# A decoder layer on one core: the context's keys and values in plain fp32 instead of three fp32r passes

## The reference

```python
kv = (key_value_states @ Wkv).reshape(B, K, 2, H, D)      # context [32, 375, 256] @ [256, 512], fp32
k = kv[:, :, 0].transpose(0, 2, 1, 3)
v = kv[:, :, 1].transpose(0, 2, 1, 3)
scores = jnp.einsum('bhsd,bhkd->bhsk', q, k) + bias
attn = jax.nn.softmax(scores, axis=-1)
out = jnp.einsum('bhsk,bhkd->bshd', attn, v)
return out @ Wo
```

## Time and profile before

| What | us |
|---|---|
| median of 3 runs (lowest, highest) | 1374.55 (1373.27, 1375.71) |
| the profiled execution | 1373.25 |
| its span in the trace | 1371.6 |
| TensorE busy | 1270.6 |
| POOL, DVE, ACT busy | 856.5, 832.5, 718.6 |

### The profile page before, as it was taken

One profiled execution on the slowest core, in us unless ns is written; L12 is line 12 of the kernel. 1 busy time (PEld: TensorE's weight loads), 2 busy tenths in 40 slices (PEclk: granted clock), 3 DMA queues, 4 the chain that ended last, 5 costly groups with the idle time before them and its releaser, 6 DMA issues. The chain is left out here.

```text
span 1371.6 us, 41710 instructions
## 1 busy us (share of the span) xinstructions
PE 1270.6 (93%) x13316; PEld 1069.9 (78%) x13317; DVE 832.5 (61%) x3821; ACT 718.6 (52%) x1827; POOL 856.5 (62%) x1597
## 2 busy tenths in 40 slices
PE   5499999999999999999999999996199999999993
PEld 3378888878878888878878878874099999999993
DVE  2257767777677767777677767765444444444441
ACT  2256666566656666566656666564044444444440
POOL 4276787778777787778777777775423544444431
PEclk9799999999999999999999999999599999999997
DMA  8910111100101111110101111000366332222224
GB/s 163 174 46 23 30 38 34 30 30 27 45 27 30 31 38 34 30 31 27 44 27 30 30 33 36 12 16 27 114 197 175 55 50 50 46 46 46 47 44 122
DMA packets 47327, 73.30 MB, mean 53 GB/s; under 512 B 6832, under 2 KB 34032, under 8 KB 47088
## 3 DMA queue, kind: packets, MB, share of 16 engines
q1 hardware_dynamic: 31408, 45.74, 12.5%
q0 software_dynamic: 15744, 25.31, 9.3%
HBM read 46.90 MB, written 27.80 MB: 54 GB/s over the span
## 5 line engine op out<-in xcount | busy, mean ns | idle before, releaser
L458 POOL TENSOR_SCALAR arena<-arena,mC 112x375 f32<-112x375 f32 x512 | 299.7, 595 | 155.0 <-DVE mC L839 153.1
L839 DVE CUSTOM_DVE_ANT_0 arena<-bank_S,arena 112x375 f32<-112x375 f32 x512 | 254.9, 545 | 113.8 <-PE bank_S L586 84.0
L1070 POOL DMA_INDIRECT acc<-y,xb x64 | 116.5, 1821 | 210.4 <-DVE y L1214 155.3
L464 POOL TENSOR_SCALAR arena<-arena,mF 112x112 f32<-112x112 f32 x512 | 202.2, 417 | 8.1 <-DVE mF L827 8.1
L693 ACT ACTIVATE arena<-bank_B 128x224 f32<-128x224 f32 (+6 forms) x260 | 101.1, 389 | 114.1 <-PE bank_B L567 54.2
L693 ACT ACTIVATE arena<-bank_A 128x224 f32<-128x224 f32 (+3 forms) x252 | 98.7, 392 | 109.2 <-PE bank_A L567 54.3
L1201 DVE SCALAR_TENSOR_TENSOR hT<-bankU,gub,gate 128x128 f32<-128x128 f32 x256 | 72.1, 344 | 101.7 <-PE bankU L1110 99.0
L721 ACT ACTIVATE pTC<-bank_Q 126x336 f32<-126x336 f32 x256 | 115.2, 450 | 34.2 <-PE bank_Q L595 24.1
L586 PE MATMUL bank_S<-arena 32*112 32x376 f32 x1024 | 116.0, 522 | 17.9 <-DVE mC L839 17.6
L1110 PE MATMUL bankG<-xbT,gwb 128*128 128x128 f32 x1024 | 126.6, 277 | 1.0 <-ACT gwb L1157 1.0
L1110 PE MATMUL bankU<-xbT,uwb 128*128 128x128 f32 x1024 | 126.0, 277 | 0.0
(11 more groups left out here) (196 smaller groups left out, 2714.2 us busy)
## 6 DMA issues: line engine op xcount, KB each, us to landing
arena<-in_l_ctxT SPq DMA_DIRECT2D x32, 378.0 KB
xb<-xs POOLq DMA_DIRECT2D x64, 129.0 KB, 3.5
arena<-in_L_ffn_gate_w SPq DMA_DIRECT2D x8, 512.0 KB
arena<-in_L_ffn_up_w SPq DMA_DIRECT2D x8, 512.0 KB
arena<-in_L_ffn_down_w SPq DMA_DIRECT2D x8, 512.0 KB
arena<-in_x SPq DMA_DIRECT2D x32, 112.0 KB, 2.0
acc<-arena SPq DMA_DIRECT2D x32, 112.0 KB, 1.9
out<-acc SPq DMA_DIRECT2D x4, 896.0 KB, 9.3
```

Source lines behind the costliest of these rows:

```text
L458: pool.tensor_scalar(z[n % NZ][:, 0:T], z[n % NZ][:, 0:T], -1.0, mC[:, n:n + 1], ALU.mult, ALU.add).then_inc(s_u, 1)
L464: m = pool.tensor_scalar(sF[r][:, j, :], sF[r][:, j, :], -1.0, mF[:, r, j:j + 1], ALU.mult, ALU.add)
L839: dve.tensor_tensor_reduce(out=z[n % NZ][:, 0:T], in0=bank[f"S{r}"][0:S, 0:T], in1=nbias[:, n, :], scale=1.0, scalar=3.0e38, op0=ALU.add, ...
L1070: pool.indirect_dma_start(out=acc[:, :], out_offset=bass.IndirectOffsetOnAxis(ap=xb[x][:, D + 1:D + 2].bitcast(I32), axis=0), in_=y2[x % 2 ...
```

## The change

Each product of the context projections is one fp32 matmul on the loaded context and the loaded weights. The tiles `cT` and `wkv`, their semaphores, the steps `ch` and `cl` and `split_weights` are gone. TensorE waits for the context's load itself, and SP waits for the four projections of the item two before. The table `PERIOD` is a new one: a different order in every engine, and items up to 5 periods ahead instead of 4.

```diff
-t9@-1 e7@-1 pv1 xn@2 x1 su2@2 xn2 su0@2 v0c e2@-1 ln2 t11@-1 u10 e4@-1 t10@-1 nrmc@-2 oncc@-2 t12@-1 t15@-1
...
+u15@-1 p7@1 t5 oc3@-2 pf@-1 v0@2 e1@-1 e0@-1 onc p5@1 wo@2 u1 u2 e3@-1 rcA@-2 nrm@1 v@3 e7@-1 t11 otc t8
...
-            cT = [s1(f"cT_{part}", [P, DC, TPAD], F32R) for part in ("high", "low")]
-            wkv = [s1(f"wkv_{part}", [P, DC, 2 * D], F32R) for part in ("high", "low")]
-            PASSES = ((0, 0), (1, 0), (0, 1))
...
                         elif step == "Lc" and b >= 2:
-                            sp.wait_ge(s_cl, b - 1)
+                            for w in ("k0", "k1", "v0", "v1"):
+                                filled_wait(sp, w, b - 2)
                             load_c(b)
...
                     def keys(o, b, B_, F_):
                         for c in range(DC):
-                            for u, w in PASSES:
-                                m = pe.matmul(B_[:, 0:T + 1], wkv[w][:, c, o * P:(o + 1) * P], cT[u][:, c, 0:T + 1],
-                                              start=(c == 0 and (u, w) == PASSES[0]), stop=(c == DC - 1 and (u, w) == PASSES[-1]))
+                            m = pe.matmul(B_[:, 0:T + 1], wkv_in[:, c, o * P:(o + 1) * P], cin[b % 2][:, c, 0:T + 1],
+                                          start=(c == 0), stop=(c == DC - 1))
...
                             for c in range(DC):
-                                for u, w in PASSES:
-                                    m = pe.matmul(B_[0:TP, k * D:(k + 1) * D], cT[u][:, c, t * TP:(t + 1) * TP],
-                                                  wkv[w][:, c, D:2 * D], start=(c == 0 and (u, w) == PASSES[0]),
-                                                  stop=(c == DC - 1 and (u, w) == PASSES[-1]))
+                                m = pe.matmul(B_[0:TP, k * D:(k + 1) * D], cin[b % 2][:, c, t * TP:(t + 1) * TP],
+                                              wkv_in[:, c, D:2 * D], start=(c == 0), stop=(c == DC - 1))
...
                         elif step in ("k0", "k1"):
-                            pe.wait_ge(s_cl, b + 1)
+                            pe.wait_ge(s_c[b % 2], 16 * (b // 2 + 1))
...
-                        elif step == "ch":
-                            act.wait_ge(s_c[b % 2], 16 * (b // 2 + 1))
-                            if b:
-                                for w in ("k0", "k1", "v0", "v1"):
-                                    filled_wait(act, w, b - 1)
-                            copy(cT[0][:, :, :], cin[b % 2][:, :, :], s_ch)
...
-                            dve.wait_ge(s_ch, b + 1)
-                            dve.tensor_tensor(cT[1][:, :, :], cin[b % 2][:, :, :], cT[0][:, :, :].bitcast(F32),
-                                              ALU.subtract).then_inc(s_cl, 1)
```

More of the change, by code:

```diff
@@ L66 @@
 PERIOD = """
-t9@-1 e7@-1 pv1 xn@2 x1 su2@2 xn2 su0@2 v0c e2@-1 ln2 t11@-1 u10 e4@-1 t10@-1 nrmc@-2 oncc@-2 t12@-1 t15@-1
-t14@-1 t13@-1 S0@1 x2Tc p8 su3@2 Lc@1 x2@-2 v1c ln3@-2 u1@1 e5@-1 ch@1 x3T@-1 e6@-1 oc0@-1 su1@2 q2m sm2@1
-e11@-1 p10 sm0@1 sm3@1 qk@3 vc@1 e9@-1 xTc@2 sT0@2 p14 x3@-2 rt@-1 sm1@1 S1@1 t1 sT3@2 t3 sT1@2 k0@2 sE2@1 p15
-pvS@2 p12 oc1@-1 e8@-1 t0 x3Tc@-2 pv2 t2 u0@1 e10@-1 p13 sE0@1 u3@1 p3@1 e14@-1 qkc@2 sE3@1 re@-2 cl@1 sE1@1
-lg@-2 ot@2 pv3 p1@1 sc@-2 p0@1 e15@-1 on@2 pf@-1 S2@1 rcA@-2 p7@1 wo@2 p2@1 k1@2 ln1@3 u4@1 v0@2 otc u7@1
-rs1@4 km@3 p4@1 u2@1 S3@1 u6@1 u5@1 onC u8@1 p6@1 k0c@1 t4 t7 p5@1 oTc@1 x2T@2 Lx@3 rs2@2 e12@-1 woc t5 u11@1
-v1@2 u9@1 oc2@-1 S4@3 t6 pv0@1 nrm@1 u15@1 q2@2 e13@-1 e3 oc3@-1 p11@1 u14@1 e1 u13@1 rcB@-2 onc@1 st@-3 v@3
-e0 xT@4 k1c@1 rs3 p9@1 pfD@-2 u12@1 sT2@3 t8
+u15@-1 p7@1 t5 oc3@-2 pf@-1 v0@2 e1@-1 e0@-1 onc p5@1 wo@2 u1 u2 e3@-1 rcA@-2 nrm@1 v@3 e7@-1 t11 otc t8
+pfD@-2 v0c e5@-1 S3@1 xT@4 vc@1 xTc@2 p6@1 oncc@-2 onC e6@-1 p4@1 v1@2 e4@-1 v1c xn2 t10 t9 u0 woc p10@1 u7
+x2Tc u4 e10@-1 oc0@-1 p11@1 e11@-1 u5 S4@3 x2T@2 km@2 q2m x1@1 nrmc@-1 e8@-1 pv0@1 q2@2 u6 p8@1 x3@-2 k0@3
+sT0@3 sE0@1 k0c@1 e9@-1 sE1@1 ln2@1 xn@3 t13 sc@-3 oc1@-1 t15 e14@-1 pv1@1 rs1@4 x3Tc@-2 e13@-1 p9@1 sT1@3
+S0@2 t14 p14@1 x3T u9 p13@1 oc2@-1 pv2@1 qkc@2 sE3@1 u11 qk@4 t12 sT3@3 re@-2 u10 x2@-1 e12@-1 rt p12@1 S1@2
+ln3@-1 rs2@1 sT2@3 e15@-1 sE2@1 p15@1 k1@3 sm0@2 u8 k1c@1 pvS@3 p2@2 sm1@2 p1@2 u14 sm3@2 rcB@-2 sm2@2 t2@1
+Lc@2 pv3@1 t3@1 rs3@-1 u13 t1@1 t0@1 lg@-1 ln1@5 su0@2 Lx@5 oTc@1 su1@2 t4@1 ot@3 e2 su3@2 p0@2 S2@2 t7@1 u12
+on@3 st@-2 su2@2 p3@2 u3@1 t6@1
 """
@@ L290, in decoder_layer @@
             s_pool = sem("pool_constants_ready")
-            s_wkv = sem("context_weights_split")
             s_fb = sem("bias_rows_filled")
@@ L302, in decoder_layer @@
             s_xn2 = sem("xn2_ready")
-            s_ch = sem("context_high_ready")
-            s_cl = sem("context_low_ready")
             s_u = sem("cross_scores_shifted")
@@ L625, in _ @@
                             pe.wait_ge(s_late, 16 * NLATE)
-                        if b == 0 and step in ("k0", "k1", "v0", "v1"):
-                            pe.wait_ge(s_wkv, 1)
                         B_, F_ = fill_wait(pe, step, b), fill_sem(step, b)
@@ L893, in set_up @@
                         link(dve.tensor_scalar(padf[:, :], iota[:, 0:E], float(R), rowf[:, :], ALU.mult, ALU.add))
-                    def split_weights():
-                        dve.wait_ge(s_late, 16 * NLATE)
-                        link(dve.tensor_copy(wkv[0][:, :, :], wkv_in[:, :, :]))
-                        dve.tensor_tensor(wkv[1][:, :, :], wkv_in[:, :, :], wkv[0][:, :, :].bitcast(F32),
-                                          ALU.subtract).then_inc(s_wkv, 1)
                     for step, b in steps:
@@ L923, in _ @@
                             statistics(1, x1[b % NX][:, :])
-                        elif step == "cl":
-                            if b == 0:
-                                split_weights()
-                            dve.wait_ge(s_ch, b + 1)
-                            dve.tensor_tensor(cT[1][:, :, :], cin[b % 2][:, :, :], cT[0][:, :, :].bitcast(F32),
-                                              ALU.subtract).then_inc(s_cl, 1)
                         elif step == "nrmc":
```

## The result

| kernel | median, us | range, runs | span of the profiled run | clock |
|---|---|---|---|---|
| before | 1374.08 | 1373.27 to 1375.71, 4 | 1371.6 | 0.969 |
| after | 1401.32 | 1399.12 to 1402.19, 4 | 1399.9 | 0.965 |

The ratio is 1.0191, 95% interval [1.018, 1.0203]: 27 us slower. Forecast were 1385 us and a range up to 1400. The sign was right, the size was less than half of what came, and the range missed by 1.3 us.

A forecast was written before the change was run, and what follows sets the result against it. TensorE was taken to bound the first stage. 31 items at +0.40 us gave 12.4; with - 1.7 + 0.3 at the start, +11.0 us, so 1385 us. Its own range was 1381 to 1391, the wider one 1377 to 1400.

The forecast's parts named there:

- ScalarE's and VectorE's copies: ACT's 32 copies of 0.84 us and DVE's 32 subtractions of 0.95 us lie beside a full TensorE; removal worth 0.
- the bare fp32 prices: Context steps on TensorE in plain fp32: key step 1.27 us, value steps 1.73 and 0.87 us.
- the borrowed 0.19 at the projection: Projection before the last value step shows 0.68 us for 0.87; the 0.19 us come back in the new order.
- DVE's 3 us for the fifth x: At the start DVE stands 3 us for the fifth x; booked at +0.3 us, at most +3.
- the moved waits in SP's queue: Context load waits for the four projections of the item two before; worth 0.
- What plain fp32 costs: Context products on TensorE: 5.14 us in fp32 against 4.70 for fp32r passes, 0.44 us more an item.
- The order: Walk through one period's 49 groups: others 23.32 us, context 5.14, together 28.46; +0.39, taken as +0.40 an item.
- The start, -1.7 + 0.3: A key step and transposes vanish in the stall before 67 us, -1.7 us; DVE's wait for x, +0.3.
- Rival 1: Context steps: no switch saved between kinds of products, so +0.95 us an item, 1401 us; chance 0.09.
- Rival 2: New order stalls TensorE: late DVE at the normalised heads, 0.3 us an item, 1394 us; chance 0.10.
- Rival 3: TensorE is not the bound; its full rows hide waits that longer products fill, 1374 us; chance 0.08.
- Even distances: TensorE rows of one kind equally far from the next start, 0.87 us for projections, taken to prove the bound.

The follow-up runs named there:

- 11: Kernel before's order with plain fp32, ScalarE's context copy put back into a tile nobody reads; period 28.60 us, ratio to before 1.0092.
- 12: Kernel before's order with plain fp32, VectorE's subtraction put back into a tile nobody reads; period 28.57 us, ratio to before 1.0095.
- 3: Changed kernel with ScalarE's last self exponential of an item moved ahead of a cross exponential; period 28.79 us, ratio to before 1.0149.
- 6: Changed kernel, self exponential first, mask-group scores moved right ahead of the first cross values; 1394.64 us, ratio to before 1.0142.
- run 1: Plain fp32 in the order of the kernel before; 1391.61 us, period 28.60 us, ratio to before 1.0095, timed again 1.010.
- 5: Changed kernel, self exponential first, two pairs of steps on tiles of 32 made neighbours again; period 29.09 us, ratio to before 1.024.
- run 8: Kernel before with the thirteenth head's transposes moved ahead of the self values; period 28.03 us, ratio to before 0.9991.
- run 2: Kernel before with its three fp32r passes, put in the new order; period 28.75 us, ratio to before 1.0132.
- 7: Kernel before with two neighbouring pairs of steps on tiles of 32 parted; period 29.31 us, ratio to before 1.0282.

## Why the prediction was wrong

**Right.** TensorE bounds the stage but for about 0.3 us an item of hidden waits; the sign; ScalarE's and VectorE's copies are worth nothing each (11, 12); the bare fp32 prices (key step 1.27, found 1.28; values 0.87, found 0.86 to 0.88; the long one 1.73, found 1.73 in the old order and 1.81 in the new); the borrowed 0.19 at the projection comes back; DVE's 3 us for the fifth x, with no bracket on TensorE behind it; the moved waits in SP's queue cost nothing, no row of TensorE waits for a context.

**The term "What plain fp32 costs", +0.44.** It was mis-sized by a little: +0.51 alone. The 5.14 us were priced with transposes behind every group. In the old order two of the four groups have another follower and take 0.09 more each, and their places in the earlier trace rows (4.89 us) already hold this; four other steps gave 0.22 back. ScalarE's rows of the kernel before show that wait (11 and 12), but the rows read for the prediction were TensorE's.

**The step that failed: "The order".** The walk through a period gave other groups 23.32 us and the context 5.14, 28.46 or +0.39 in all. Measured in the changed kernel, the other groups take 23.43 and the context 5.45 (the key step before the self values 1.48 for 1.27, the long value step 1.81 for 1.73), together 28.88. Against fp32 in the old order the new one costs 0.28, where the walk gave it nothing. The walk took its prices from pairs in the trace of before, and the four dearest new pairs have no row there: key step before self values 1.48 (transposes behind: 1.28), two transposes before cross values 0.34 (0.19), four transposes before scores 0.53 (0.43), self transposes before scores 0.48 (0.39). For two of them a near row stood there: the four transposes take 0.57 and the self transposes 0.48 before cross values, which run on tiles of 32 as the scores do. Of the 0.28, the hidden wait behind ScalarE is 0.07 to 0.09 (3) and one visit more to tiles of 32 is 0.14 (6). By the rows the second visit more costs as much, and the wait of the key step behind DVE, 0.15 in run 1, is gone in the new order, so these two about cancel; neither was shown by a run of its own, since mending the second pair made a bank wait (5). Some 0.05 stays open; the long value step alone takes 0.08 more in front of its new follower.

**The start, -1.7 + 0.3.** It was +0.6 to the self values, and -0.4 in the second profile. The stall swallowed what was put in front of it, as said, but the group left behind it (a key step) was priced at 1.27 and took 2.67 at the 1.2 GHz level, and 1.86 in the second profile. The row to price from was the scores at 67.11 in the earlier trace rows: 1.61 us for what takes 0.90 elsewhere. Of the span's 28.3 us, 4.3 lie before the fifth self values (2.4 of them three periods), 21.7 in the 27 periods from there, 0.7 on the way to the last cross values, and 2.8 between these and the first expert transposes (948.71 to 989.80 before, 975.41 to 1019.26 after); stage 2 is 1.2 shorter. The prediction had no term for the end. The stretch of 2.8 belongs to the new order: it is 43.9 to 45.0 us in all six traces with that order, with either arithmetic, and 41.1 to 42.3 in those with the old one, but for run 8 (43.4). What in the order makes it is open.

**The rivals.** Rival 1 gave 1401, the time that came, by the wrong road: its saved switch would have made the old order with fp32 cost 0.95 an item, not 0.51. Rival 2 (a late engine) was right in kind: 0.07 to 0.09 us behind ScalarE at the self values, not 0.3 behind DVE at the heads. Its test, a bracket, could not have found it. Rival 3, with the warning of the Trainium skill (Trainium Kernel Development and Optimization, section Performance Expectations) that matmul busy time is a bad measure, had a point that I argued away: the rows hide waits, 0.22 us behind ScalarE and 0.10 behind DVE in the kernel before, and fp32 costs only 0.13 in the new order with its longer wait for the exponential; yet TensorE was the bound for the rest. Even distances did not prove that rows hide nothing: the waits come back in nearly every period and are even as well, and the 0.39 that the walk used for transposes before a key step holds one of them. The range was cut at 1400, though a mis-sized term and a hidden wait can come together; both did.

## What to carry to other kernels

Price a group on TensorE by what stands behind it, and when a new order makes pairs that the old trace does not have, book them at the dearest like pair, here 0.15 us for each separate visit of the engine to tiles of 32. Keep groups on such tiles side by side, but look at which bank each neighbour then takes: two of the five such swaps lost 0.5 to 0.9 us an item to a bank. Where matmul ends are modelled, a full row of TensorE hides waits of 0.1 to 0.3 us. Look for the other engine's last read of the bank or last write of the input: where the group starts at the same small lag behind it in every period, it waits, and moving that step shows it.

## What the runs showed of the hardware that was not expected

- Plain fp32 (two instructions a product, 0.32 and 0.216 us each at 376 and 256 columns) beats four fp32r passes by 0.61 us for 3040 columns an item, some 0.1 of it a wait; against three passes it loses 0.13 to 0.51, by what stands around it.
- Going from full tiles to 32-wide ones costs 0.09 us, going back 0.05 to 0.06 in the transposes behind, going on among them nothing. The key step before the value step pays 0.09 too (1.37 against 1.28), and there both are full tiles: the tiles are not the whole rule.
- The clock came back at different times after a stall that ended at 67 us, in one kernel too: in 69 to 71 us it was granted 0.50 and 0.73 in two profiles of the changed kernel, 0.68 in the kernel before and 0.50 in run 2, which has fp32r products there as well. So it differs from execution to execution, and nothing here ties it to the arithmetic.
- A group of TensorE that waited for a bank starts 0.05 to 0.06 us behind the recorded end of the read that freed it, with a bracket (runs 5 and 7) or without one (11 and 12).
- The kernel before read 3 to 5 us higher in some sets of runs than in others, once on the same chip.
